# Moving the block of value products from behind the fourth to behind the second score tile of a k tile in a two-layer attention kernel

## The reference, cut to what matters

```python
# layer 0
scores = einsum('bhqd,bhkd->bhqk', Q, K) / sqrt(16) - 0.1 * abs(tq - tk)
attn = softmax(scores, axis=-1)
out = einsum('bhqk,bhkd->bhqd', attn, V)
x = x + tanh(g_xattn[0]) * (out @ Wo.T + bo)
# layer 1: Q, K, V with relu and no bias, no time term, no Wo
x = x + tanh(g_xattn[1]) * out
```

## Time and profile before

| what | value |
|---|---|
| runs, us | 834.14, 835.5, 832.04; median 834.14 |
| span of the profiled execution, us | 834.1 |
| PE busy | 737.3 us, 88% |
| DVE busy | 581.4 us, 70% |
| ACT busy | 440.8 us, 53% |
| POOL busy | 296.2 us, 36% |

### The profile page before, as it was taken

How to read it: one execution, slowest core, us unless ns; L and a number is a source line. 1 busy time by engine, 2 the same in 40 slices (tenths; PEclk the granted TensorE clock), 3 DMA queues, 4 the chain that set the end, 5 groups by cost and what they waited for, 6 DMA issues and landing times.

```text
span 834.1 us, 12041 instructions
## 1 busy us (share of the span) xinstructions
PE 737.3 (88%) x4096; PEld 428.6 (51%) x4096; DVE 581.4 (70%) x1126; ACT 440.8 (53%) x840; POOL 296.2 (36%) x348
## 2 busy tenths in 40 slices
PE   5897599999998998999768999899999886899991
PEld 3443234343432676777523334333353775799981
DVE  5473689999970489265758899799943537577775
ACT  2222488888887535665016888687853422233330
POOL 2121255555554234755000000755423304233322
PEclk9897699999999999999877999999975989899996
DMA  8497355454444431002722255522012202111100
GB/s 298 112 180 219 108 179 180 169 170 155 166 166 155 152 101 51 1 1 73 173 62 81 71 175 169 149 77 64 18 46 83 92 1 90 39 48 44 42 15 21
DMA packets 51357, 87.52 MB, mean 105 GB/s; under 512 B 8598, under 2 KB 16792, under 8 KB 51297
## 3 DMA queue, kind: packets, MB, share of 16 engines
q1 hardware_dynamic: 44320, 72.06, 28.2%
q0 software_dynamic: 4576, 11.54, 5.3%
q10 hardware_dynamic: 2400, 3.15, 1.1%
HBM read 45.29 MB, written 41.63 MB: 104 GB/s over the span
## 4 chain that ended last, share of the span: by engine, by line
PE 56%; issue 11%; DVE 11%; DMA 8%; POOL 6%; SPq 4%; ACT 3%; POOLq 0%; DVEq 0%; ACTq 0%
PE ps_out L712 14%; PE ps_a L698 10%; PE ps_wide L593 6%; DVE row_max L1395 5%; PE ps_misc L698 5%; PE ps_a L522 4%; DMA out_x<-sorted_rows,ids 3%; PE ps_a L830 3%; SPq L438 2%; PE ps_wide L688 2%; POOL sorted_rows L1287 2%; PE ps_wide L894 1%; POOL hid_lo L1255 1%; PE ps_out L844 1%; ACT probs L1020 1%
## 5 line engine op out<-in xcount | busy, mean ns | idle before, releaser
L1395 DVE TENSOR_REDUCE row_max<-ps_wide 128x2 f32<-128x1024 f32 x256 | 301.1, 1219 | 34.0 <-PE ps_wide L593 27.8
L1020 ACT ACTIVATE probs<-ps_a 128x512 f32<-128x512 f32 x342 | 191.5, 602 | 57.4 <-PE ps_a L698 49.4
L593 PE MATMUL ps_wide<-stack_k,stack_q 48*128 48x512 f32 x512 | 155.1, 472 | 15.2 <-DVE row_max L1395 11.0
L698 PE MATMUL ps_a<-stack_q,stack_k 62*128 62x512 f32 (+1 forms) x342 | 142.3, 467 | 13.1 <-ACT probs L1020 10.1
L712 PE MATMUL ps_out<-probs,vals 128*17 128x512 f32 x1024 | 142.2, 631 | 0.5 <-POOL probs L1214 0.5
L698 PEld LDWEIGHTS ps_a<-stack_q,stack_k 62*128 62x128 f32 (+1 forms) x342 | 61.9, 194 | 102.4 <-ACT probs L1020 69.3
L1020 ACT ACTIVATE probs<-ps_misc 128x512 f32<-128x512 f32 x170 | 102.4, 603 | 19.4 <-PE ps_misc L698 15.5
L1214 POOL TENSOR_TENSOR probs<-probs,fixes_sb 128x512 f32<-128x512 f32 x64 | 82.2, 1284 | 82.5 <-ACT probs L1020 82.5
L593 PEld LDWEIGHTS ps_wide<-stack_k,stack_q 48*128 48x128 f32 x512 | 63.0, 191 | 50.5 <-DVE row_max L1395 20.2
L698 PE MATMUL ps_misc<-stack_q,stack_k 62*128 62x512 f32 (+1 forms) x170 | 78.8, 463 | 2.9 <-ACT probs L1020 2.9
L1199 POOL TENSOR_SCALAR max_neg<-row_max 128x16 f32<-128x16 f32 x32 | 9.2, 289 | 158.5 <-DVE row_max L1395 137.3
(11 more groups left out here) (214 smaller groups left out, 1326.7 us busy)
## 6 DMA issues: line engine op xcount, KB each, us to landing
rows_sorted<-blank SPq DMA_DIRECT2D x17, 1040.0 KB, 5.0
planes_k<-planes SPq DMA_DIRECT2D x32, 256.0 KB, 3.8
planes_q<-planes SPq DMA_DIRECT2D x32, 256.0 KB, 3.5
stack_q<-planes_q SPq DMA_DIRECT2D x64, 128.0 KB, 2.8
stack_k<-planes_k SPq DMA_DIRECT2D x64, 128.0 KB, 2.8
w_raw<-in_L_W SPq DMA_DIRECT2D x6, 1024.0 KB, 5.1
stack_q<-planes_q SPq DMA_DIRECT2D x64, 64.0 KB, 2.7
stack_k<-planes_k SPq DMA_DIRECT2D x64, 64.0 KB, 2.6
```

The lines of the kernel that those rows point to most:

```text
L593: mm(raw_slot(l, ("pair", g, p))[:, i * S:(i + 1) * S], stack_q[at, slot(g, c) + q * P:slot(g, c) + (q + 1) * P], stack_k[at, slot(g, c):s ...
L698: mm(score_slot(("tile", n))[:], stack_k[at, slot(g, c) + k * P:slot(g, c) + (k + 1) * P], stack_q[at, slot(g, c):slot(g, c) + S], start=T ...
L1020: do(probs[n % PROBS[l]][:, j, :], score_slot(("tile", n * HG + j))[:], ACT.Exp, scale=0.25).then_inc(exp_done, 1)
L1395: v.tensor_reduce(row_max[:, g % 2, :, p], raw_slot(l, ("pair", g, p))[:].rearrange("p (i k) -> p i k", i=2), AX, ALU.max).then_inc(sem(f" ...
```

## The change

`weigh` of a k tile is issued after the second score tile and no longer after the fourth. It still takes the k tile that is two behind, in both layers. `turn_maximum` and `turn_out` of k tile 1 now follow the fourth score tile directly. No instruction is added or taken away, on any engine; the order of the four other engines stays the same.

```diff
@@ -723,6 +723,8 @@
                                 for_maximum(l, ahead, 2 * k + c, 1, True)
                                 for_maximum(l, ahead, 2 * k + c, 0, False)
                             scores(g, k, c, 1)
+                            if c == 0:
+                                weigh(g * QT + k - BEHIND)
                             if l == 1 and (g, k, c) == (G - 2, 2, 0):
                                 turn_n3(1)
                         if l == 1 and (g, k) == (G - 2, 2):
@@ -730,7 +732,6 @@
                         if l == 1 and (g, k) == (G - 2, 3):
                             count(0)
                             route_logits(1)
-                        weigh(g * QT + k - BEHIND)
                         if l == 1 and (g, k) == (G - 1, 0):
                             count(1)
                             total(0)
```

## The result

The change makes the kernel slower: 845.82 us (median of 4 runs, 842.45 to 846.44) against 833.09 (4 runs on the same chip, 825.85 to 835.5), a ratio of 1.0162 with an interval of 1.0126 to 1.0199. A second measurement, with six runs, gave 1.0140 (1.0102 to 1.0178), 843.82. The forecast was 849 with a range of 837 to 856. Ratios are taken from the fast executions; two far slower ones are left out of them, 882.68 us of `only_k1` and 909.37 us of `tail_k2`, with mean granted clocks of 0.769 and 0.725 in place of 0.92 to 0.94.

The account below looks back on a forecast made before the run. It took a 2.60 us loop of score, exponential, score and products as the bound, with DVE close behind. Terms 10.8 + 1.8 + 0.9 + 0.6 + 1.1 = 15.2 on 834.1 gave 849 us, range 837 to 856.

Parts of the forecast that it names:

- The mechanism: At k tile 2, p4 takes p3's bank and waits for its reduction: products' interval 3.72 us against 3.25.
- The first term: Groups 2 to 13 of both layers, without layer 1's group 7: p4's wait costs 23 x 0.47 = 10.8 us.
- The loop of 2.60: Score, exponential, score three banks on, products, score: stays 2.60 us per k tile, so the rotation costs nothing there.
- The second term: Layer 1's groups 9 to 13: `update3` delays DVE, a later interval is 3.07 to 3.14, +0.35 five times, 1.8 us.
- The third: Layer 1's group 7: the stall before group 8 swallows its longer waits, but p0's later reduction costs +0.9 us.
- The fourth: Group 1 of each layer, no turned output: `keep_out` binds at 3.30 against 3.01, 2 x 0.3 = 0.6 us.
- The fifth: Ends of both layers' attention: +0.66 us in layer 0, +0.5 in layer 1 at the low clock, together 1.1.
- No loss: Rival: p3's reduction ends before p4 is due at k tile 2, so no wait; 833 or 837 us; chance 0.11.
- DVE as the bound throughout: Rival: late reductions push the next group's, so every group pays 0.8 us, 856 us in all; chance 0.12.
- The clock: Rival: repeated short PE waits lower the clock in places, k tile 4.04 us not 2.60; 861 or more; chance 0.03.
- 0.05 a group, where only `keep_out` binds: Lower bound of p4's wait per group: `keep_out` alone gives 3.30 us against 3.25.
- What is not symmetric is k tile 1: Placed the loss at k tile 1, where products no longer stand between p3 and p4: +0.47 us a group.

Follow-up runs that it names:

- only_k1: The kernel before with the products moved early at k tile 1 alone: 836.83 us, ratio 1.0041 to the kernel before.
- tail_k2: The kernel before with the new order only in layer 1 from group 14's k tile 2 on: 832.69 us, ratio 1.0008 to the kernel before.
- undo_k1: The changed kernel with the move undone at k tile 1 alone, products again between p3 and p4: 841.97 us, ratio 1.0106 to the kernel before.
- tail_only: The kernel before with the new order only in layer 1's groups 14 and 15: 828.2 us, ratio 0.9954 to the kernel before.
- tail_last: The kernel before with the new order only in layer 1's group 15: 830.79 us, ratio 0.9956 to the kernel before.
- nokeep_before: The kernel before without `turn_out`, `normalise` and all but the last `keep_out`: 818.73 us, ratio 0.9828 to the kernel before.
- p4_late: The changed kernel with p4 issued behind the products of k tile 2: 859.07 us, ratio 1.0339 to the kernel before.
- after_again: The changed kernel measured and profiled again without an edit: 843.82 us, ratio 1.0140 to the kernel before.

## Why the prediction was right, and where a size was off

**The mechanism** held as written. p4 takes p3's bank and waits for its reduction (forecast 3.03 after the products' start, with PE's in-order wait behind it); the interval was put at 3.72 and is 3.71. The turns came 0.1 sooner than put (k tile 2's first tile at 2.30 and not 2.40), which lies inside the wait and changes nothing. The period, 11.49 in the expectation of `undo_k1`, is 11.48. The first term, 23 x 0.47, measures 0.45 to 0.46 a group. The loop of 2.60 elsewhere is untouched, POOL's fix kept its cover in layer 0 (no wait at the intervals shown), and `normalise` fell out of the way.

**The second term** (layer 1's late groups, 5 x 0.35): intervals of 3.09 inside the 3.07 to 3.14 worked out, periods longer by 0.76 to 0.80 against 0.82. The delay shows already at group 6, once more than I counted (11.18 became 11.93).

**The third** (group 7, +0.9) measures +0.6 in one profile and -1.6 in the other. The stall moves with the landing of its transfer (3.15 and 2.32 against 3.01). Behind the 3.15 the clock was low for some 3 us (0.83 over 540 to 550 us), and around the 2.32 it stayed at 1.00, which is worth 1.7 us more. So this term can't be read to better than 2 us. In the first profile another DMA wait stood in group 4, and it alone makes that period 12.58 in place of 11.48:

```profile
494.22 0.49 PE L698 MATMUL ps_misc<-stack_q,stack_k 50*128 50x512 f32 x1 [1.22 <-DMA stack_q<-max_rows]
...
543.58 0.49 PE L698 MATMUL ps_a<-stack_q,stack_k 50*128 50x512 f32 x1 [3.15 <-DMA stack_q<-max_rows]
```

**The fourth** (group 1, twice 0.3): 3.37 against 3.01, so 0.36 each. `keep_out` as the next wait in line was right.

**The fifth was the step that failed**, in its second half, layer 1's end "at the low clock", put at +0.5. It took the low clock of the old trace as given for the new one, and its 2.2 and 1.2 for the tiles at that clock stand in none of the rows that it names. In both profiles of the changed kernel the stretch ran 14 us shorter at 1.2 GHz, and the end of layer 1 took 6.8 us less, not 0.5 more. Why the clock came back sooner is open (above). Layer 0's end cost 1.4 in place of 0.66; part of this is that group 14 has no pairs, so its turned maximum comes 0.27 earlier than the period counts.

**Not in the sum at all** was the start of layer 1: +2.6. The clock was at 1.2 GHz for about 17 us there, before for 10. Not all of it need be the change's: `tail_only`, `tail_last` and `tail_k2`, with the old order there, took 19.8 us for this stretch, with some 14 us of low clock, against 18.3 before and 20.9 after. Windows of the kernel before and of the changed one:

```profile
445.00:450.00 5.00, 5.00 (x20) 2.39 (x20) 4.47 (x5) 4.00 (x9) 0.00 (x0) 0.50 0.01 3
450.00:455.00 5.00, 5.00 (x31) 2.10 (x23) 3.26 (x4) 2.58 (x6) 0.24 (x1) 0.77 0.08 25
```

```profile
455.00:460.00 5.00, 5.00 (x24) 1.60 (x16) 3.22 (x3) 2.24 (x5) 0.68 (x3) 0.50 0.13 41
460.00:465.00 5.00, 4.77 (x28) 2.27 (x24) 3.25 (x3) 3.20 (x8) 0.00 (x0) 0.79 0.40 116
```

The groups' terms were right within 1 us, but for the third in the second profile, and these two together gave -4.2 (2.6 less 6.8) where the sum had +0.5. With that the sum is 10.5, against 12.2 to 12.7 between medians; what is left, 2 us, is within what whole runs vary by. That the total lies under 849 is the doing of these two terms, which nobody forecast: with +0.5 in place of -4.2 the two medians of 843.82 and 845.82 would be 848.5 and 850.5. So the groups' terms carry the forecast, and its nearness doesn't rest on the two cancelling. The profiled pair differs by 6.5 only, or 10.3 without the 3.8 that its stretch ahead of the first score was shorter.

**The rivals.** No loss fell: 1.42 us were to lie between p3 and p4, measured are 1.31 (150.03 to 151.34), and 2.05 are needed (150.03 to 152.07 is 2.04). DVE as the bound throughout fell: layer 0's periods stay at 11.48 for eleven groups, and the reductions have caught up within each. Its price came true where it was expected, in the late groups alone. The clock stayed at 1.00 in the groups but for the stall in front of group 8 and for layer 1's first groups, which had a low clock before, too:

```profile
150.00:160.00 10.00, 9.77 (x64) 4.07 (x60) 8.65 (x10) 7.52 (x17) 4.82 (x7) 1.00 0.50 170
540.00:550.00 10.00, 6.85 (x37) 2.25 (x33) 5.86 (x7) 4.49 (x9) 6.46 (x8) 0.83 0.43 115
```

This answers to the earlier trace rows, and to both figures. The rival was not empty, though: `undo_k1` shows it. In its late groups two waits follow each other, and in three of the five the clock then falls for some microseconds:

```profile
587.03 0.19 PEld L593 LDWEIGHTS ps_wide<-stack_k,stack_q 48*128 48x128 f32 x2 [0.90 <-DVE row_max L1398]
588.16 0.19 PEld L593 LDWEIGHTS ps_wide<-stack_k,stack_q 48*128 48x128 f32 x2 [0.71 <-DVE row_max L1398]
588.82 1.57 PE L712 MATMUL ps_out<-probs,vals 128*17 128x512 f32 x8
...
592.65 1.05 PE L712 MATMUL ps_out<-probs,vals 128*17 128x512 f32 x8
```

The products take 1.57 in place of 1.05, and the next follow after 3.83, where it is 2.31 in the late groups with a full clock. There are two of those, right behind: the same two waits (0.90 and 0.70 at 600.26 and 601.39, 0.91 and 0.72 at 611.96 and 613.09) left the clock at 1.00. So the waits alone don't decide it. The Trainium skill ("TensorE: Matmul & The Clock Gate", A second HAM failure mode: psum-queue depth-cycling) names such short idles between groups as a way into the low clock; here the trace agrees in three late groups of this kernel, with a clock of 0.74 over 590 to 595 us. It disagrees in the two other late groups and in the changed kernel, where one wait of 0.55 a group, and in the late groups one of 0.90 and one of 0.55 3.7 us apart (596.07 and 599.75), leave the clock at 1.00.

**What is weaker than I wrote**: the lower bound of "0.05 a group, where only `keep_out` binds". It holds for a kernel in which nothing but p4's wait is taken from the changed one, with `keep_out` at 3.30; it is 3.37, so 0.12 a group. And the attribution to k tile 1 ("What is not symmetric is k tile 1") is too narrow, since the move there alone costs 0.13 and its undoing leaves 0.15. The size comes from the places of the products at k tile 1 and behind it together.

## What to carry to other kernels

Before work is moved out from between two users of a ring of buffers, write down the ring's next item and what the old user still needs: start, the reader's latency and its duration. If the moved work was what covered that time, the move turns it into a wait of the in-order engine, though not one instruction more is issued. When a wait is removed, count on the next one just under it (here 0.3 us each, three deep), and compare the periods of repeating groups rather than whole runs, whose clock stretches vary by more than many such effects. An order that costs in the steady state may still pay in a drain, where the work runs out; here two placements there gained 0.4 to 0.5% and a third nothing, so it has to be tried.

## What the runs showed of the hardware that was not expected

- A switch from a score tile to value products took 0.31 to 0.33 us where the score stood right behind its neighbour, and 0.42 where it stood alone. That is 0.1 us of the 0.3 by which `only_k1` fell short of its forecast.
- PE's clock is low in two stretches, at the start and the end of layer 1's attention, in every profile. The one at the end begins in all profiles but one (`nokeep_before`, 1.8 us ahead) 2 to 8 us behind the first small matmuls of the routing (L635 in the changed kernel), and lasts 10 us in `p4_late` and 17 to 31 us in the others, whose work there is nearly the same; at half speed each us of it costs half a us. Neither gaps in PE nor the order of the products explains its length in all runs. It stays open.
- In the attention itself a wait of 0.41 in each k tile, or one of 0.55 a group, left the clock at 1.00. Waits of 0.90 and 0.71 that ended 1.1 us apart were followed by 1.2 GHz in some groups of `undo_k1` and not in others. A stall of 3.0 to 3.15 us was followed by it, one of 2.32 us in `after_again` was not, and one of 1.90 us in `undo_k1` was (0.50 over 505 to 510 us). So no length of a wait seen here tells by itself what the clock does.
